# Gated experts of the last layer: two 32-row bands of gates, so that two chunks get their gates from two products side by side

## The reference, cut to what matters

```python
x_flat = x.reshape(Bx * Tx, H)
logits = x_flat @ gate_w.T
scores = jax.nn.softmax(logits, axis=-1)
_, topk_ids = jax.lax.top_k(scores, NUM_EXPERTS_PER_TOK)      # 2 of 8
in_topk = jax.nn.one_hot(topk_ids, E, dtype=x.dtype).sum(axis=1)
w = scores * in_topk
gu = jnp.einsum('nh,eih->nei', x_flat, experts_gate_up)
g, u = (gu[..., :I], gu[..., I:])                             # I = 176
h = jax.nn.silu(g) * u
expert_out = jnp.einsum('nei,ehi->neh', h, experts_down)
out = jnp.einsum('neh,ne->nh', expert_out, w)
shared = jax.nn.silu(x_flat @ shared_gate_w.T) * (x_flat @ shared_up_w.T) @ shared_down_w.T
shared_weight = jax.nn.sigmoid(x_flat @ shared_expert_gate_w.T)
out = out + shared_weight * shared
```

## Time and profile before

| | |
|---|---|
| median of 3 runs | 3561.42 us (3557.74 to 3566.69) |
| profiled execution, its own time | 3553.97 us |
| span of the profiled execution | 3552.1 us |
| PE, DVE, ACT, POOL busy in the span | 96%, 70%, 57%, 35% |
| stage of the change | from about 2951 us to the end |
| PE in 2990 to 3030 us of it | busy 39.05 of 40 us |
| DVE there | busy 30.83 of 40 us |

### The profile page before, as it was taken

How to read it: one execution, slowest core, us unless ns; L and a number is a source line. 1 busy time by engine, 2 the same in 40 slices (tenths; PEclk the granted TensorE clock), 3 DMA queues, 4 the chain that set the end, 5 groups by cost and what they waited for, 6 DMA issues and landing times. The chain is left out here.

```text
span 3552.1 us, 99744 instructions
## 1 busy us (share of the span) xinstructions
PE 3412.4 (96%) x43493; PEld 2808.9 (79%) x43493; DVE 2473.8 (70%) x4946; ACT 2033.0 (57%) x3467; POOL 1244.1 (35%) x923
## 2 busy tenths in 40 slices
PE   7999899999999899999999989999999998999999
PEld 6888788887888555788888878878888886777777
DVE  8977555555667799666666667766666666777776
ACT  4445555554666688455555545555555555566564
POOL 1322133334554233222222223322222224555555
PEclk9999999999999999999999999999999999999999
DMA  3000000001000000000000000010000000000000
GB/s 110 11 11 11 1 1 1 1 1 38 15 15 8 1 1 1 23 9 7 7 9 7 5 22 1 1 47 9 7 7 9 7 5 1 7 7 13 7 7 13
DMA packets 15488, 41.03 MB, mean 12 GB/s; under 512 B 2959, under 2 KB 4687, under 8 KB 14158
## 3 DMA queue, kind: packets, MB, share of 16 engines
q1 hardware_dynamic: 15054, 34.64, 3.2%
HBM read 30.44 MB, written 4.19 MB: 10 GB/s over the span
## 5 line engine op out<-in xcount | busy, mean ns | idle before, releaser
L708 ACT ACTIVATE projL<-bank 128x512 f32<-128x512 f32 (+1 forms) x640 | 371.3, 601 | 646.0 <-PE bank L291 630.4
L511 POOL TENSOR_TENSOR probL<-probL,invL 128x1024 f32<-128x1024 f32 x160 | 304.5, 1903 | 1196.5 <-DVE invL L821 1196.5
L1704 POOL TENSOR_TENSOR h_loM<-hM,h_hiM 126x512 fp32r<-126x512 f32 x224 | 290.3, 1296 | 254.7 <-ACT h_hiM L1830 252.0
L598 PEld LDWEIGHTS bank<-valuesL,probTL 64*64 64x64 f32 x10240 | 277.7, 133 | 60.9 <-issue 55.0
L810 DVE TENSOR_REDUCE neg_maxL<-bank 128x16 f32<-128x1024 f32 x160 | 195.9, 1224 | 183.7 <-PE bank L617 152.9
L598 PE MATMUL bank<-valuesL,probTL 64*64 64x128 f32 x10240 | 316.4, 272 | 4.4 <-ACT probTL L718 4.4
L1403 PEld LDWEIGHTS bank<-w2T,hM 128*128 128x128 f32 x2304 | 276.8, 192 | 39.3 <-ACT hM L1458 24.1
L1403 PE MATMUL bank<-w2T,hM 128*128 128x128 f32 x2304 | 283.4, 276 | 16.2 <-ACT hM L1458 16.2
L1458 ACT ACTIVATE hM<-bank,ahead_scales 128x512 f32<-128x512 f32 x288 | 183.8, 684 | 189.3 <-PE bank L291 189.0
L825 DVE COPY valuesL<-bank 128x512 f32<-128x512 f32 x320 | 213.1, 679 | 107.2 <-PE bank L291 101.3
L818 DVE TENSOR_REDUCE totalL<-probL 128x16 f32<-128x1024 f32 x160 | 194.8, 1217 | 122.4 <-ACT probL L723 122.1
(11 more groups left out here) (309 smaller groups left out, 9050.0 us busy)
## 6 DMA issues: line engine op xcount, KB each, us to landing
ct0L<-in_ctxP SPq DMA_DIRECT2D x24, 192.0 KB, 2.5
ct1L<-in_ctxP SPq DMA_DIRECT2D x24, 192.0 KB, 2.5
x<-in_x SPq DMA_DIRECT2D x4, 1024.0 KB, 10.9
out<-x SPq DMA_DIRECT2D x8, 512.0 KB, 2.6
nct<-in_ctxP SPq DMA_DIRECT2D x16, 192.0 KB, 2.4
ahead_second<-in_L0w SPq DMA_DIRECT2D x2, 1152.0 KB, 18.1
ahead_second<-in_L3gate SPq DMA_DIRECT2D x1, 882.0 KB
ahead_second<-in_L3up SPq DMA_DIRECT2D x1, 882.0 KB
```

What stands on the lines that cost most here:

```text
L511: nc.gpsimd.tensor_tensor(segments(prob[:, slot, :]), segments(prob[:, slot, :]), per_segment(inv[:, slot, :]), ALU.mult).then_inc(prob_re ...
L598: last = nc.tensor.matmul(o_bank[b * SEQ:(b + 1) * SEQ, t, u * D:(u + 1) * D], probT[t * SEQ:(t + 1) * SEQ, 2 * s + u, b * SEQ:(b + 1) * SEQ],
L708: nc.scalar.activation(proj[:, u, :], rot.bank(step, f"P{u}")[0:rows, :], ACT.Copy, scale=scale if paired and u % 2 == 0 else 1.0).then_in ...
L1704: nc.gpsimd.tensor_tensor(h_lo[:, a % SLOTS, :], h[:, a % 3, :], h_hi[:, a % SLOTS, :].bitcast(F32), ALU.subtract).then_inc(lo_ready, 1)
```

## The change

The gates are now laid out by token in two bands of 32 columns (`gates` is 4 x 2 x 32 wide). Each band holds the nine high parts in its columns 0 to 8 and the nine low parts in 9 to 17; DVE makes both before the turn, with a copy that rounds and a subtraction. After the turn, `gT` has 64 rows, two equal bands, and ACT alone keeps it; `gates_rest` is gone. `owner` has 64 rows: band 0 for the even chunks and band 1 for the odd ones, half as many columns. `spread_gates` runs once for two chunks, with a product from each band, 32 rows by 126, into the two banks. It stands behind `down` of the even chunk, and waits until `h` of the chunk before is made, since it overwrites both banks.

```diff
-        gates, top = sb("gatesM3", [P, G, CTX]), sb("topM3", [P, G])
+        BANDS, BAND = 2, 32
+        gates, top = sb("gatesM3", [P, G, BANDS, BAND], F32R), sb("topM3", [P, G])
+        gate_of = sb("gate_ofM3", [P, G, R])
...
-        owner = sb("owner_M3", [CTX, C, F], F32R)
-        gT = [sb(f"gT{s}_M3", [CTX, GT], F32R) for s in range(2)]
+        owner = sb("owner_M3", [BANDS * BAND, C // BANDS, F], F32R)
+        gT = [sb(f"gT{s}_M3", [BANDS * BAND, GT], F32R) for s in range(2)]
...
                     if a > 1:
-                        pe.wait_ge(h_ready, a - 1)
-                    nc.tensor.matmul(g_bank[a % 2][0:F, :], owner[:, n, :], gT[i % 2][:, :], start=True, stop=True)\
-                        .then_inc(spread, 1)
+                        pe.wait_ge(h_ready, a)
+                    for u in range(BANDS):
+                        band = slice(u * BAND, (u + 1) * BAND)
+                        nc.tensor.matmul(g_bank[u][0:F, :], owner[band, n // BANDS, :], gT[i % 2][band, :],
+                                         start=True, stop=True).then_inc(spread, 1)
...
-                        spread_gates(i, n)
                         if n >= LAG:
                             down(i, n - LAG)
                         elif i > 0:
                             down(i - 1, C + n - LAG)
+                        if n % BANDS == 0:
+                            spread_gates(i, n)
...
-                        lambda: ch.link(nc.vector.tensor_tensor(gates[:, :, 1:9], eq[:, :, :], probs[:, :, :], ALU.mult)),
-                        lambda: ch.link(nc.vector.tensor_copy(gates[:, :, 32:41], gates[:, :, 0:9])),
+                        lambda: ch.link(nc.vector.tensor_tensor(gate_of[:, :, 1:R], eq[:, :, :], probs[:, :, :], ALU.mult)),
+                        lambda: ch.link(nc.vector.tensor_copy(gates[:, :, :, 0:R], in_bands())),
+                        lambda: ch.link(nc.vector.tensor_tensor(gates[:, :, :, R:2 * R], in_bands(),
+                                                                gates[:, :, :, 0:R].bitcast(F32), ALU.subtract)),
                     ]
                     return steps
-
-                def gates_rest(j):
-                    dve.wait_ge(gT_hi_kept, j + 1)
-                    nc.vector.tensor_tensor(gT[j % 2][32:41, :], bank[32:41, :], gT[j % 2][32:41, :].bitcast(F32),
-                                            ALU.subtract).then_inc(gT_ready, 1)
```

More of the change, by code:

```diff
@@ L110, in __init__ @@
         self.down = second[0:126, 3528:5320].rearrange("p (n d) -> p n d", d=D)
-        self.owner = second[0:CTX, 5320:7084].rearrange("p (n f) -> p n f", f=126)
+        self.owner = second[0:64, 5320:6202].rearrange("p (n f) -> p n f", f=126)
     def load_attention(self, sp, tag, loaded):
@@ L1660, in gated_moe @@
             sem(n) for n in ("router_done", "logits_kept", "shifted_ready", "e_ready", "chain"))
-        gates_turned, gT_hi_kept, gT_ready = (sem(n) for n in ("gates_turned", "gT_hi_kept", "gT_ready"))
+        gates_turned, gT_ready = sem("gates_turned"), sem("gT_ready")
         gate_done, up_done, spread, down_done = (sem(n) for n in ("gate_done", "up_done", "spread", "down_done"))
@@ L1685, in _ @@
             def _(pool):
-                nc.gpsimd.memset(gates[:, :, :], 0.0).then_inc(gates_zero, 1)
+                nc.gpsimd.memset(gates[:, :, :, :].bitcast(F32), 0.0).then_inc(gates_zero, 1)
                 pool.wait_ge(c.ahead.experts_in, 64)
@@ L1689, in _ @@
                                         c.ahead.owner.rearrange("p n f -> p (n f)"),
-                                        c.one[0:CTX, :].to_broadcast([CTX, C * F]), ALU.mult).then_inc(owner_kept, 1)
+                                        c.one[0:BANDS * BAND, :].to_broadcast([BANDS * BAND, C // BANDS * F]),
+                                        ALU.mult).then_inc(owner_kept, 1)
                 def split_hi(j, slot):
@@ L1728, in turn_gates @@
                 def turn_gates(j):
-                    pe.wait_ge(chain, (j + 1) * 20)
+                    pe.wait_ge(chain, (j + 1) * 21)
                     for s in range(G):
-                        last = nc.tensor.transpose(bank[0:CTX, s * P:(s + 1) * P], gates[:, s, :], c.ident[:, :])
+                        last = nc.tensor.transpose(bank[0:BANDS * BAND, s * P:(s + 1) * P],
+                                                   gates[:, s, :, :].rearrange("p b r -> p (b r)").bitcast(F32), c.ident[:, :])
                     last.then_inc(gates_turned, 1)
@@ L1840, in keep_gates @@
                     act.wait_ge(gates_turned, j + 1)
-                    nc.scalar.activation(gT[j % 2][:, :], bank[0:CTX, :], ACT.Copy).then_inc(gT_hi_kept, 1)
+                    nc.scalar.activation(gT[j % 2][:, :], bank[0:BANDS * BAND, :], ACT.Copy).then_inc(gT_ready, 1)
                 def keep_output(i):
@@ L1888, in shift_logits @@
                 def shift_logits(j):
-                    ch = Chain(dve, chain, j, 20)
+                    ch = Chain(dve, chain, j, 21)
                     dve.wait_ge(router_done, j + 1)
@@ L1898, in shift_logits, with in_bands @@
                     return ch
+                def in_bands():
+                    return gate_of[:, :, :].unsqueeze(2).to_broadcast([P, G, BANDS, R])
                 def route(j, ch):
@@ L1902, in route @@
                         lambda: ch.link(nc.vector.tensor_scalar(sigmoid[:, :], e[:, :, 8], 1.0, None, ALU.add)),
-                        lambda: ch.link(nc.vector.reciprocal(gates[:, :, 0], sigmoid[:, :])),
+                        lambda: ch.link(nc.vector.reciprocal(gate_of[:, :, 0], sigmoid[:, :])),
                     ] + softmax8(nc, ch, e, probs, total) + first_of_largest(
@@ L1935, in _ @@
                 ch.close()
-                gates_rest(0)
                 for i in range(NG):
@@ L1957, in _ @@
                             add_output(i - 1)
-                        if n == 13 and i + 1 < NG:
-                            gates_rest(i + 1)
                         if i == 0 and n < 3:
@@ L2588, in lay_out @@
     o["L3down"] = chunks(a["L3_ffn_shared_down_w"].T, a["L3_ffn_experts_down"].transpose(0, 2, 1)).transpose(1, 0, 2)
-    owner = np.zeros((CTX, 14 * 126), np.float32)
+    owner = np.zeros((32, 14 * 126), np.float32)
     for row in range(1760):
         g = 0 if row < 352 else 1 + (row - 352) // 176
-        owner[[g, 32 + g], row] = 1.0
-    o["L3owner"] = owner.reshape(CTX, 14, 126)
+        owner[[g, 9 + g], row] = 1.0
+    o["L3owner"] = owner.reshape(32, 7, 2, 126).transpose(2, 0, 1, 3).reshape(64, 7, 126)
     o["L3router"] = np.concatenate([a["L3_ffn_gate_w"], a["L3_ffn_shared_expert_gate_w"]]).T
```

## The result

The changed kernel takes 3578.41 us (median of 16 runs, 3571.84 to 3607.49), the kernel before 3559.57 (16 runs, 3556.04 to 3570.5): the ratio is 1.005, with an interval of 1.0037 to 1.0064. It is slower by about 19 us. The profiled execution after has a span of 3575.3 us, 23.2 more than before.

The account below looks back on a forecast made before the run. PE, busy nearly all of 3552.1 us, was taken to bound the kernel; 20.4 (fifteen groups) + 1.05 (last group) - 2.0 (start) = +19.4 us on the median 3561.42 gave 3581 us, own range 3571 to 3590, with rivals 3557 to 3595.

Parts of the forecast that it names:

- the sum: Whole kernel: 20.4 for fifteen groups, 1.05 for the last, 2.0 off at the start: +19.4 us.
- A pair costs 0.62 us: PE, two band products between full products: 0.62 us against 0.464 for two full ones, dearer by 0.15.
- The rival of a free shape: PE at the pairs: change of shape costs nothing, 0.25 us a pair; +1 us, 3562; chance 0.21.
- the serial one: PE at the pairs: the bands run one after the other, 0.22 us more per pair; +34, 3596; chance 0.09.
- The layout of a group: Gated experts, PE from `h` of chunk 5: chunk 13 0.95 us late, 0.41 more after; a group 1.36 longer.
- The waits, 0.3, 1.1 and 0.3: PE waiting for `h` at chunks 6, 8 and 10: some 25 us in all in place of 15.9.
- The period, 37.5 predicted: Gated experts, time from group to group: 37.5 us in place of 36.15.
- DVE's held steps move along with `h`: Routing on DVE: POOL follows `h` through ACT, so the pattern of 1.1 us steps moves along with DVE's chain.
- The start: Ahead of the loop and first group: 1.20 us off `shiftedM`, 0.68 and 0.1 off `gates_rest`; 2.0 us gained.
- the predicted 1.05 for the last group: Last group, no routing and no such waits: seven pairs at 0.15 us, 1.05 us lost.
- The faster rival: DVE's chain gets shorter, waits go, with a cheap change of shape: -42 us, half of it 3541; chance 0.14.

Follow-up runs that it names:

- full_pairs: Changed kernel, pairs where they are, but each product over 96 rows of one table, so the array shape never changes: 3576.76 us, ratio 1.0046.
- single_bands: Changed kernel with one band product per chunk, at the old place with the old wait for `h`: 3621.9 us, ratio 1.0185.
- bands_thin_low: Changed kernel with POOL's low part of `h` over 8 of its 512 columns: 3554.65 us, a single time.
- bands_late_split: Changed kernel with the low part of the next input (xT_lo) at chunk 11 in place of 5: 3570.01 us, ratio 1.0025.
- before_behind_h: Kernel before, with xT_lo at chunk 11 and the small routing steps right behind `h` at chunks 5 to 10: 3535.91 us, ratio 0.9916.

## Why the prediction was right

Forecast 3581 us, measured 3578.41; forecast difference 19.4, measured 18.8. That the difference is met within 0.6 us is in part luck: the interval of the ratio reaches from 13 to 23 us, and the two profiled executions, on which the terms were read, differ by 23.2, with 2.6 us in the first group that the sum did not have. What held is the mechanism, read term by term.

- **A pair costs 0.62 us.** Held: 0.63, read above. Emptying 0.09 and late load (predicted 0.31 behind the last `down`, measured 0.32), 0.43 to the next product, 0.34 to its successor: all from 64-row tiles of another stage, and right for 32 rows by 126. The shape alone costs 0.39 a trip, 0.38 by the terms (0.09 + 0.10 + 0.31 + 0.11 - 0.232). The rival of a free shape is refuted by this, and the serial one by the single row for both bands and by the equal time behind one band and two.
- **The layout of a group.** Predicted chunk 7 at 0.48, 9 at 6.39, 11 at 11.48, 13 at 16.74; measured 0.47, 6.35, 11.42, 16.67. The waits, 0.3, 1.1 and 0.3, came as 0.18, 1.00 and 0.19; 23.0 us in all for about 25. The period, 37.5 predicted, is 37.48 (+1.33 for +1.36).
- **What that layout rested on without a test** was that DVE's held steps move along with `h`. They did: `sigmoid` has a median of 1130 ns after, 1155 before. The experiments show how much hung on it: to free `sigmoid` alone is worth 0.8 us a group, nearly as much as chunk 13 came late.
- **Which part is to blame** I had not split. In place, pairing makes 0.98 of the 1.33 and the shape 0.35, because the waits swallow the shape's cost at two or three pairs. With DVE hardly held it turns round: of 1.59 about 1.15 is the shape (7 x 0.164) and 0.45 the two waits.
- **The start.** Predicted -2.0, measured -1.5: the first pair is at 2966.35 instead of 2966.85, though the earlier stages ended 1.0 us later in this execution. `owner` takes 1.65 us, `shiftedM` 0.19, and PE's first wait fell from 3.58 to 2.38, about as predicted. But the last three of the eight router products ahead of it last 0.36 us each in place of 0.26, at the lower clock, and so PE came to that wait 0.33 later.
- **A term that was missing: the first group.** There, the token-scale steps on DVE, 3.3 us of them, hold up `h` of chunk 5, and a pair 6/7 that needs it waits longer than chunk 7 did. The pair in the timeline of the changed kernel:

```profile
2985.81 0.79 PE L1762 MATMUL bank<-gT_M,owner_M 32*126 32x512 f32 x2 [3.64 <-DVE hM L1970]
```

Busy times by stretch (columns as in the earlier trace rows) of the changed kernel around it:

```profile
2975.40:2986.00 10.60, 6.96 (x31) 4.90 (x29) 7.40 (x16) 5.94 (x10) 5.71 (x5) 0.98 0.00 0
2986.00:2993.00 7.00, 7.00 (x19) 5.17 (x20) 4.12 (x11) 2.98 (x6) 2.55 (x2) 0.55 0.00 0
```

The last of these stretches in the kernel before:

```profile
2986.00:2993.00 7.00, 6.25 (x26) 4.79 (x27) 6.42 (x15) 4.00 (x8) 3.89 (x3) 1.00 0.00 1
```

After a pause of 3.64 us the granted clock is 0.55 over 7 us, most of it at the lower of the two levels (1.2 of 2.4 GHz), and the products up to 2992.24 are 0.43 us apart; before, with 2.07 us of pause ahead of it, the same stretch has 1.00. `full_pairs` (a pause of 2.38 us, then 0.54 over 7 us) and `single_bands` (2.24, then 0.62) have it too, so it needs neither the bands nor the pairs. Chunk 13 of this group starts 3.03 us later than before, from a pair that started 0.50 earlier: 3.53, of which 0.95 was in the sum, so 2.6 were not. The profile's difference then adds up: 1.0 for the earlier stages, -1.5 for the start, 2.6 here, 15 x 1.33, and the predicted 1.05 for the last group make 23.1 of 23.2.
- **The faster rival** named the right mechanism on the wrong kernel: less hold on DVE does bring much (up to 0.84% with the gates of before), but the change doesn't bring it.

The Trainium skill, "SBUF — State Buffer", section "Who interferes with whom", states that a VectorE instruction with two SBUF inputs contends with a GpSimd instruction that reads SBUF, that a copy, a cast or a `tensor_scalar` can contend in its two-port mode, and that whichever of the two is issued first blocks the other until it is done; that a reduction never contends on this chip, and that one SBUF input outside those modes is free. The rows above agree: 1.12 us for `sigmoid` and 1.12 for L1558 beside a POOL operation that started first, 0.19 for the reduction, no hold for `h` and `t`. Applied before the first experiments, it would have made me ask which steps meet POOL before I spread them.

## What to carry to other kernels

In this kernel a small matmul between full ones pays for the change of tile shape both ways, 0.39 us a trip, so a pack has to save more than that. Where GpSimd and VectorE share a loop, try to put VectorE's steps with two SBUF inputs, its small copies and its scalar steps into the gap before GpSimd's operation can start, and reductions, reciprocals and steps that read PSUM beside it; here that brought the period from 35.30 to 34.74 us. Lay a moved product out on the time axis, wait by wait: the busy time of the gate products fell by 41 us, and the kernel lost 19.

## What the runs showed of the hardware that I had not expected

- The hold follows the kind of the step, not its size: 4 columns by `tensor_scalar` take 1.12 us, 128 x 32 elements of a reduction 0.19 beside the same kind of POOL operation.
- The hold locks in: since POOL follows `h` at a fixed distance (1.43 us) and the held step delays the next `h`, spread steps collide once per chunk, period after period.
- The length of a pause on PE alone doesn't tell what the clock does next. In the first group, 3.64 us of pause (changed kernel) were followed by some 6 us at half clock and 2.38 (`full_pairs`) and 2.24 (`single_bands`) by a granted clock of 0.54 and 0.62 over 7 us. 3.06 (`bands_thin_low`), 2.88 (`bands_late_split`) and no more than 1.89 us (`before_behind_h`) were followed by 0.76, but 2.07 (before) by 1.00. Each is one execution; what decides is left open.
- Pauses of 0.2 to 1.0 us at the pairs of the later groups left the granted clock at its upper level.
